# Loading a tile's decays as two DMAs of 64 rows, in a kernel with a written order of work

## What is computed

```python
x = x + 0.5 * _L0_ffn_ref(_layernorm(x), ...)
x = x + _L0_attn_ref(_layernorm(x), ...)
x = x + 0.5 * _L0_ffn_ref(_layernorm(x), ...)
```

```python
C = ft[:, :, None, None] * C + it[:, :, None, None] * (vt[..., :, None] * kt[..., None, :])
n = ft[..., None] * n + it[..., None] * kt
ht = jnp.einsum('bhde,bhe->bhd', C, qt)
denom = jnp.maximum(jnp.abs(jnp.einsum('bhd,bhd->bh', n, qt)), 1.0)[..., None]
```

## Time and profile before

| | |
|---|---|
| time, median of 3 runs | 1038.27 us (1033.71 to 1042.24) |
| profiled execution, its own time | 1040.67 us |
| its span | 1038.6 us |
| mean granted TensorE clock | 0.939 of full speed |
| TensorE busy | 890.4 us (86%) |
| VectorE busy | 627.3 us (60%) |
| ScalarE busy | 358.7 us (35%) |
| GpSimd busy | 244.5 us (24%) |
| DMA queue of SP, share of 16 engines | 25.7% |

### The profile page before, as it was taken

The page is one execution under the profiler, slowest core; times in us unless marked ns, Lnnn a source line. Parts: engine busy times, 40 slices in busy tenths (PEclk is TensorE's granted clock), DMA queues, the critical chain, the costliest instruction groups (busy, mean ns, idle before and its releaser), DMA issues.

```text
span 1038.6 us, 30736 instructions
## 1 busy us (share of the span) xinstructions
PE 890.4 (86%) x12744; PEld 846.2 (81%) x12744; DVE 627.3 (60%) x1502; ACT 358.7 (35%) x716; POOL 244.5 (24%) x234
## 2 busy tenths in 40 slices
PE   3858579998859997998999988799887987699998
PEld 3848568998759996998889988799876976698998
DVE  5454367684826756576666748466574786477742
ACT  5262042432503334242523335143342442123431
POOL 2022123220312202332312213331142043321110
PEclk9978679999989999999999999899898988899999
DMA  8013322213233101322224113331032223330000
GB/s 260 29 37 114 95 82 87 64 54 80 60 104 106 46 19 51 106 90 66 58 69 135 42 54 78 115 89 49 10 98 76 73 85 102 107 91 2 1 12 31
DMA packets 64392, 76.03 MB, mean 73 GB/s; under 512 B 10782, under 2 KB 46750, under 8 KB 64256
## 3 DMA queue, kind: packets, MB, share of 16 engines
q1 hardware_dynamic: 64256, 74.08, 25.7%
HBM read 56.75 MB, written 17.30 MB: 71 GB/s over the span
## 4 chain that ended last, share of the span: by engine, by line
PE 48%; DMA 16%; issue 15%; SPq 8%; DVE 7%; ACT 3%; POOL 2%; ACTq 0%; DVEq 0%; POOLq 0%
PE bank L1092 14%; PE bank L1093 12%; PE bank L1094 12%; DMA dm<-f_scratch 9%; SPq L438 4%; DMA parts_scratch<-pc 2%; DMA arena<-parts_scratch 2%; SPq L456 2%; PE bank L1250 2%; PE bank L1127 2%; DMA f_scratch<-fTz 1%; DMA c_scratch<-cum 1%; PE bank L1310 1%; PE bank L1329 1%; PE bank L1289 1%
## 5 line engine op out<-in xcount | busy, mean ns | idle before, releaser
L1092 PE MATMUL bank<-wo_hi,r_h 128*128 128x256 f32 x512 | 151.2, 295 | 19.4 <-DVE r_l L835 17.4
L643 ACT ACTIVATE r_h<-bank 128x512 fp32r<-128x512 f32 x128 | 76.4, 597 | 252.9 <-PE bank L1127 181.5
L1092 PE MATMUL bank<-xT_hi,wi_hi 128*128 128x256 f32 x512 | 151.2, 295 | 2.5 <-DVE r_l L835 2.4
L1093 PE MATMUL bank<-wo_hi,r_l 128*128 128x256 f32 x512 | 147.2, 288 | 0.0
L1094 PE MATMUL bank<-wo_lo,r_h 128*128 128x256 f32 x512 | 147.1, 287 | 0.0
L1093 PE MATMUL bank<-xT_hi,wi_lo 128*128 128x256 f32 x512 | 146.6, 286 | 0.0
L1094 PE MATMUL bank<-xT_lo,wi_hi 128*128 128x256 f32 x512 | 146.4, 286 | 0.0
L835 DVE SCALAR_TENSOR_TENSOR r_l<-bank,r_h 128x512 fp32r<-128x512 f32 x128 | 87.4, 684 | 87.0 <-ACT r_h L643 86.8
L1012 DVE TENSOR_TENSOR_SCAN dm<-dm,diag 128x512 f32<-128x512 f32 x64 | 78.6, 1229 | 67.2 <-DMA dm<-f_scratch 67.1
L1092 PEld LDWEIGHTS bank<-wo_hi,r_h 128*128 128x128 f32 x512 | 100.0, 195 | 23.4 <-issue 19.8
L1092 PEld LDWEIGHTS bank<-xT_hi,wi_hi 128*128 128x128 f32 x512 | 100.3, 196 | 4.7 <-DVE r_l L835 3.1
(11 more groups left out here) (157 smaller groups left out, 2152.5 us busy)
## 6 DMA issues: line engine op xcount, KB each, us to landing
dm<-f_scratch SPq DMA_DIRECT2D x64, 256.0 KB
arena<-parts_scratch SPq DMA_DIRECT2D x96, 128.0 KB, 3.3
...
x<-in_x SPq DMA_DIRECT2D x16, 256.0 KB, 3.0
...
```

Source lines behind the costliest of these rows:

```text
L643: nc.scalar.activation(flat(r_h[:, n]), U[use % 2][:], ACT.Relu).then_inc(f_rh, 1)
L1092: nc.tensor.matmul(dst, lh, rh, start=first, stop=False, **more)
L1093: nc.tensor.matmul(dst, ll, rh, start=False, stop=False, **more)
```

## The change

E_ issues two DMAs for a unit in place of one. Before, one DMA had a source of 2 rows, each repeated 64 times (2 x 64 x 512), and all 128 partitions as its destination. Now each half `m` is a DMA of its own: the source is the one row of that half, repeated 64 times (64 x 512), and the destination is 64 partitions. Both count 16 on the same semaphore, so that D_ (and F_, which overwrites `f_scratch` two blocks later) waits for 32 a unit where it waited for 16. The bytes are the same, and no other instruction is added or removed.

```diff
@@ F_ (SP)
-                            sp.wait_ge(d_fb[g], 16 * len(range(g, UNITS * (b - 1), DMBUFS)))
+                            sp.wait_ge(d_fb[g], 32 * len(range(g, UNITS * (b - 1), DMBUFS)))
@@ E_ (SP)
-                        src = f_d[b % 2, j, :, GH * g:GH * (g + 1)].rearrange("m h t -> m (h t)")
-                        sp.dma_start(dm[:, n % DMBUFS], src.unsqueeze(1).to_broadcast([2, TH, GH * TH])).then_inc(d_fb[n % DMBUFS], 16)
+                        for m in range(2):
+                            src = f_d[b % 2, j, m, GH * g:GH * (g + 1)].rearrange("h t -> (h t)")
+                            sp.dma_start(dm[TH * m:TH * (m + 1), n % DMBUFS], src.partition_broadcast(TH)).then_inc(d_fb[n % DMBUFS], 16)
@@ D_ (VectorE)
-                    dve.wait_ge(d_fb[n % DMBUFS], 16 * (n // DMBUFS + 1))
+                    dve.wait_ge(d_fb[n % DMBUFS], 32 * (n // DMBUFS + 1))
```

The table ORDER is redrawn for all five engines. Each letter occurs as often as before; most pieces move by a few places. Its first row for SP:

```diff
-        H 7A F X E F C A E 2A E 4K E 2A 2K 2E 2K 2E 6A F E F E C X 2A E K A 2K E K E A E 2A 3K E K 6A E 2A F E F A E A K E 2K C E K 2O X K 2A K E K E K E 7A E
+        H 7A F X F E C E A E A 4K E A E 2A 2K E K E K E 6A F E A K F X 2E 2A C K A K A K 2E A K E 2K E K 7A E A F K A K E F K E A E C O A K O X K A K E 2K 3E
```

More of the change, by code:

```diff
@@ L93 @@
     "PE": """
[L94 to L101, removed]
@@ L102 @@
-        U G U V U M 2U V 2U S V U V U G 2U Y S 2U V G V U V U 2M 2U Y 2U 2Y 3M G S U 2Y S U M G U 2S Y M G U M U Y M G U Y 2U Y V U M 2S M 3U V Y U V U Y U V
-        U Y M S M S G M 2U V U Y 2U Y V Y 2M S V S M V 2U Y G U Y S M S Y M 3U M 2V Y U Y V Y U 3M 2U Y U Y V U V G V U G 4U V U V U V G 3U G U V G U V G U V
-        5U V U V U G U 2V G 3U V 2U G V U G 2U 2V 5U 2V 4U 2V 4U V 2U 3V""",
-    "DVE": """
[L106 to L116, removed]
@@ L117 @@
-    "ACT": """
[L118 to L124, removed]
+        3G U G 5U V 2U V 2U 2V 4U V U V U 2V 2G 5U G U G 2U G U G 7U V 2U V 2U 2V 4U S U V S Y V 2U M 2V M 2S M 2Y M G 2S Y G 3U M 2U M U M Y S U S G 2Y M U G
@@ new lines @@
+        M U G 2U G M Y M 4U Y 2U Y V 2U V M 2U 2V Y U Y 3U V 2U G 2V S G V 4U V 2U V Y U V U G U S M U G U V U G V U G V S 2M S 3U V 2U V 3U 2V 2U Y 2U V 3U V
+        G 2V G U Y U Y U M 3U M S U M G Y U Y M G Y 2S G U S M U M U G 4U Y V Y 3U V U 2M Y S 2V M U Y 2U Y 2U V S 2U G U 3V 2U G 3U V M U V 2U V S G Y M U G
+        S 3U G V U G 2V 4U V 3U M U V U 2V 3U V G U V 2U G Y V U V U Y U Y 3U M S M S M S Y G M U Y M G Y S 2U G M 2U G 3U M Y V 3U Y M U Y V U M V Y 2U Y V U
+        V 3U G U V U V G V 2U 2S U Y 2U V U V U V U G 2U V G U M S U G M S M V G U V 5U 2V 4U 2V 2U G 3U V G V Y U V U V Y 2U Y 3U M 2S 2M S G U Y U Y G M S Y
@@ new lines @@
+        U M G 2U G M 3U Y 3U Y 2U V Y 2M V M U V U Y V 2U Y 2U V U G V U S V U V M 2U G 2U V Y U V U V S U G 2U G V 2U 2S G M V M U G V 4U V 2U V U V U Y V G
+        3U V 3U V U 2V G U Y 3U Y 2U S 3M S G Y M U Y M Y S G U M G U M 2U Y G U S 4U V Y 2U Y V U V 2S 2M 2U Y V U Y V 4U G U V G 2V 4U 2M 2S U V U Y U 2V U
+        G M 2U G U V G S 2U G 2V Y 4U M U 2V 4U 2V U G U V U Y 3U 2V U G V Y U M 4U S M U S Y G U M Y G Y S M G 2U M G 8U V Y V U Y S 2M Y V S M V Y 4U V Y 3U
+        V G V 2U G V 3U V 2U V U M V G 3U Y U G V U 2S M 2V 2U M 2U Y 2U Y M Y M G S M U Y G S Y 2U S M S Y M G U M U Y G M 2U Y U Y V 2U S 2M S V 3U Y V Y V
@@ new lines @@
+        4U M Y 2U 2M 2S V G Y 2U Y V Y 2M 2V 2S M U Y 2U Y G M Y 2U V U S 2M V Y U Y V M S Y U 2M U Y 2U Y V U V G V U G 4U V U V U V G 3U G U V G U V G U V
+        5U 2V 2U V G U V G 4U V G U V U G U V U V 5U V U V U V U V 6U V U 3V""",
+    "DVE": """
+        2G H 3G 3H 2G 3H G H R 2H R 2H 2R H 3R G R 3H 2R H 3G 2H 3G R 2G R G R H 3R G 2R 2H R 2G R H 2R H G 2R 2H 2R D 3R D P R P Y R D G D Y 2R G Y G P Y G D
+        Y P G D 2G R G R Y G P 2R Y G P D 2R Y 2R Y D Y G P Y R P G Y 2R G Y 2R G Y R 2Y 2R D 2G R Y D Y R Y R G Y G R G R G 2R 2G 2R 2G 2R P R G 7R G 2R Y R
+        D R G 2R G R D P 2G 2R P R Y 2G Y R P G 2D 4R D 2R G Y R G R Y 2R Y G Y R G R G R G Y R P Y R G Y R G P Y R Y R G 2R G Y P R Y R D G Y R P R D Y G P R
+        G 2Y R Y D 2G 3R P G 3R D 4R G R G R G R 2G 2R G R P 3R G 2R G 2R Y G 2R G R D Y P R 2G D Y R D R G 2R G R D G R 2G Y 2R G R Y G Y 3R Y R P Y R P Y R
+        G Y R Y G Y 2R G 2R G P Y R Y D P 2G 2R 5Y G R Y R G R G R G R 2D 4R P G R Y R P 3R G R 2G R G 2R D 3R G R D R G R G 2R 2G 2R Y R G 2P G R G R Y D 2R
+        D R G R Y R G D 2R Y R G R Y G R G Y R G R 2P R 2Y G R Y R G Y 2R G 2R G 2Y R Y R P D Y G P Y R D Y R Y R G R G Y 2G R 2D R G P 7R G 3R 2G R 2G Y 3R G
+        2R P G 4R G R D G R P R G R G D G Y R G R Y 3R Y D P 2R G R 2G R G R G Y R G D R Y R Y R Y P R Y P Y G Y 2R Y P G Y 2R G 2R G Y 2R D Y R D G Y P G Y R
+        Y D Y G 2R Y 2G 2R P G 2R P G 2R D 3R D R G 2R G P G R G Y 3R G R Y 2R Y G 2R G 2R G 3R 2G P G D R G R P D 2R Y R Y R D G R G 2R 2G R G R Y R G R Y R
+        Y R D R P Y G R Y G Y R G Y 2R G R P 2R P 2Y R 2Y R G D Y 2D 2R G P Y G P R Y 2G R G R G 5R G R 2G 4R G 6R G D Y R Y 3R P 2G 2R P R Y R D R G R G Y R
+        G 2Y R D R 2Y P G Y D R P Y G Y D Y 2R P G Y R Y G 2R Y P 2Y G R D P Y R G D Y R P D R G Y R 2G 2Y R D Y P Y R P Y D Y R Y G D R Y R Y P R P Y 2R D R
+        G Y R Y 2R Y R G Y P D Y R Y P 2R G Y R G 2R Y R Y G R G 2R G 3R G 3R 2G R G 2R G 4R G 4R G R G 2R G 2R 2G R 2G 2R G 2R G R G 2R G 11R""",
@@ new lines @@
+    "ACT": """
+        H 6G H 2G 6H G 3H 2R 4H 3R H 2R 4H R H 6G 2H 2R 2H R 3G 3R G 2R A R Z G R G A G R G R H 2R 2A Z H G Z 8R Y 6G 3R Z R 2G 4R A 2R Y G A 3G R 2G 2R G 2R
+        Y R 2A 3R Y R G R 4G R G 5R 2G R 2G R G R G R G R Z G 2R G 4R 2G R G R Y 2R 3G 3R 2Z 6R A G R 3G A Y 2G R 2G A 3R G R Y Z 3R Y 2R A 4G R G 2R Z 3R G
+        3R 6G R G R G 3R G Z 4R Z R 2G R G R 3G R Y 3R Z 5R A 2R 3G A Y 3G R 2G 3R 2A G R Y 2R Y 2R 3G R 2G 3R G 2R 2Z 4R Z 4G 2R 2G R 2G 2R G 2R Z R G R G R
+        2G R G R G Y 10R A G R 2G A 3G Y R 2G R A 2R G R Y A 4R Y R G R 4G 4R G 4R 5G R G R 2G 2R Z R G 4R 3G Y 2R 2G 2R G 4R 2G 3R G R A R Z G R Y A G Z G R
+        2G A 3R G Y R A 3R Y R Z R G R 4G R G 7R 6G 2R 2G 2R Z R G R Z 3R 2G R G Y R G Z G 2R G 3R Z 6R A G R 2G Y A 3G R 2G 3R G A R A 2R Y 2R Y 2R 5G R G 6R
+        Z 3G R G 2R Z G R G 6R Y 4R A 2R 3G A 3G Y R 2G R A 2R Y G 2Z A 3R Y 3R 2G Y R 2G Z G Z 2R Y Z 2R G 3R Y 2R Z R Y 3R 5G R G 5R 4G R 2G 2R G R G 2R G
+        3R G R 5G 2R 2G R G 9R""",
@@ L125 @@
     "POOL": """
-        H 4G 2A G A Q A 2W Q W Y W Y G Y W G Y A W A Y 2W G A 2Y Q G Y W G A W 2G W Q Y W G 2Y G 2A Y 2W A 2Y 2W Y W G Q G A W 3G Y Q W Y W G W Y G A Y W A W
-        Y W A 2Y 2G 2W A G Q Y Q W Y G Y 2G 2W Y G 2A W Y G Y W Y W A Y G W A W G W 2G Y 2Q G Y W G Y W A W Y A Y W A W Y G W 2Y W A Q G Q G W G Y G W Y G W Y
-        G W 2A Y G 2Y W A W Y G W G A W G Y Q W Q W G Y A Y W Y A 2W A 2Y G W Y W A Y W Q G Q Y G Y 2W 2Y 3W 2Y W Y 6G""",
+        H 4G 2A G 2A Q 2W Y W Q W Y 2G W Y A W A Y 2W Y A 2Y 2G Q W G W A Y 2G W Y Q Y W G Y 2W G 2A Y G A W Y W 2Y W G Q G Q A G W Y G W Y G W G Y W A Y W A
@@ L129 @@
+        G Y 2W Y A Y G W A Y W Q G Y G 2W Q Y 2G Y G 2A 2W G 3Y W A W Y W A G W G W G Y 2Q W 2G Y G Y A 2W Y A Y W 2A W 2Y 2G W 2Q G Y 2W G Y W Y 3G W Y 2A W
+        3Y W A W A G Y G 2W G Q G Y W Q W Y G A Y A 2W 2Y W Y A W G Y A W Y 2Q W Y G W G Y W Y W Y W Y W Y W Y 6G""",
     "SP": """
-        H 7A F X E F C A E 2A E 4K E 2A 2K 2E 2K 2E 6A F E F E C X 2A E K A 2K E K E A E 2A 3K E K 6A E 2A F E F A E A K E 2K C E K 2O X K 2A K E K E K E 7A E
-        2F A 2E A K O K A C A E O X K E K E A 3K 2E K 7A E K F 3E 3A K O K A F A C O X K E K 2E 2K E K 6A E K A F 2A 2E A K F 2K E C O E O K X 2A K 3E 2K E 7A
@@ L132 @@
-        F K 2A E K A 2E 2K O A K F E A K E C E K E K 5A E 2A K 2A O F K 2E K A F E A C A K E 2K 2E O 2K 2E 5O""",
+        H 7A F X F E C E A E A 4K E A E 2A 2K E K E K E 6A F E A K F X 2E 2A C K A K A K 2E A K E 2K E K 7A E A F K A K E F K E A E C O A K O X K A K E 2K 3E
+        6A F 2E F C 3A O A E K E K O K X E K E K 2A K 2E 2K 6A F E A K E 2A K A E O E K F E K O X 2A C 2K E K 2E K 6A K 3A F K E A E K 2E F K O C 2A K O E X
+        2E K E 2K E 6A K A F A E A K A 2E F C O 2K 2A K 2E K E 2K 2A E 3A E 2A F K 3A E K F E C A 2E 2K E O K A E 3K O 2E 5O""",
```

## The result

| | before | after |
|---|---|---|
| time, median | 1040.26 us (4 runs, 1033.71 to 1043.10) | 935.10 us (4 runs, 934.78 to 939.06) |
| ratio, 95% interval | | 0.9006, 0.8954 to 0.9057 |
| span of the profiled execution | 1038.6 us | 936.9 us |
| TensorE busy / idle | 890.4 / 148.2 us | 865.0 / 71.9 us |
| mean granted clock | 0.939 | 0.980 |

The account below looks back on a forecast made before the run. TensorE's idle time and lower clock, caused by decay loads on two of sixteen DMA engines, were taken as the bound. 1040.7 - 19 - 31 - 18 + 8 = 981 for the profiled execution, so 978 us forecast, range 942 to 1012.

Parts of the forecast that it names:

- Step 1: Decay loads into dm: both halves run on 16 engines and land in 3.9 us, against 8.73 alone or 17.39 queued.
- rival of the one source row: Decay loads: one row limits the rate whatever the engines, a load takes 14 us, kernel 1096 us; chance 0.05.
- rival of the serializing halves: Decay loads: each half gets only the old engines, so the pair takes 9.3 us, kernel 1050 us; chance 0.05.
- Steps 2 and 3: TensorE's idle gaps: 19 us from S_ waits for arena, 31 us from nine gaps behind VectorE's waits for decays.
- the next releaser: TensorE's nine gaps behind decay waits: another wait follows closely, so 1 us was left at each.
- Step 4: TensorE's work at half clock behind eleven gaps, 43.2 us: up to 21.6 us come back, 18 taken.
- Step 5: SP's queue: 64 more issues, 34 us on SP alone, mostly hidden by its waiting; full 34 if cover were gone.
- Step 6: Redrawn instruction order, most pieces moved a few places: a loss of 8 us, bounds 16 gained to 40 lost.
- more than forecast: Whole kernel: the redrawn order fills what fast loads leave, all marked gaps and 16 us more go, 937 us; chance 0.12.

Follow-up runs that it names:

- e6_outer4: After, with the 64 repeats of each half's one source row written as 4 x 16; 952.8 us, ratio 0.9169 to before.
- e6_outer8: After, with the 64 repeats of each half's one source row written as 8 x 8; 937.1 us, ratio 0.9019 to before.
- e1_loads_only: After with the ORDER table of before, so only the split loads differ from before; 944.5 us, ratio 0.9080.
- e8_one_wide: After with one 128-row load a unit from 16 source rows, each half's row stored 8 times; 939.1 us, ratio 0.9057 to before.
- e7_beside: After plus, behind each unit's two loads, one DMA of the old 2 x 64 shape into a spare DRAM buffer; 1025.9 us, ratio 0.9900 to before.
- e4_rows_48_16: After with each half cut again into 48 and 16 rows, four DMAs a unit; 935.4 us, ratio 0.9021 to before.

## Why the prediction was right in direction and wrong in size

**Step 1, the load.** Right. Share 0.12 to 0.14 at an outer size of 2, proportional up to 8; landing 3.6 us for the pair against 3.9. That after has all 16 engines, as the step says, stays unproven. The rival of the one source row is dead: `e6_outer4` and `e6_outer8` read one row with 4 and 8 engines and the share grows in step. So is the rival of the serializing halves: `e1_loads_only` takes 944.5 us where before takes 1040.9. The Trainium skill's rule against two transfers to disjoint partition halves (DMA: Bandwidth & Descriptors, "Rules for kernel authors") supposes that either half is spread over all 16 engines, and so is the one transfer in its place; here the one had two. Where the one is wide, the rule fits: `e8_one_wide` (939.1) and after (935.1) are the same within their intervals. With the Trainium skill's rule on the number of engines (same page, "Why a DMA increments its semaphore by 16 and not by 1") the traces agree: 0.14, 0.25 and 0.48 for outer sizes of 2, 4 and 8, and 0.12 for 62 rows. Two of the rivals' sums are off by 2 us: 1040 + 48 + 10 is 1098 and not 1096, and 1040 + 7 + 5 is 1052 and not 1050. Nothing hangs on it.

**Steps 2 and 3, the idle time.** Mis-sized: I forecast 19 + 31 = 50 us and `e1_loads_only`, which has the old order, gained 68.9 over its whole span. The gaps that I had marked were 26.6 + 40.2 = 66.8. The marking was right, and the discounts were not: the 8 us taken off the S_ gaps and the 9 us left at nine gaps for "the next releaser". Looked up one by one, the three S_ gaps lost 25.6 us in place of 19, and the nine others 39.1 in place of 31; 2.1 us are left where I had left 17. So no next releaser stood behind the decays that would have held TensorE up by more than 1 us. The other 4.3 us lie in gaps that I had not marked; what gave them is open, though `e7_beside` shows that two held engines can delay the stores of the parts too (SP's wait for `pc`), which no gap carried by name.

**Step 4, the clock.** Mis-sized: 18 us forecast, 27.0 measured (busy time, `e1_loads_only`). I took 43.2 us of TensorE's work behind eleven gaps and then a sixth off the 21.6 they promise. But behind 100 us TensorE did 76.9 us of work at the lower level, and 16.3 in `e1_loads_only`: 60.6 us moved up. The rest of them lay behind small gaps that I had not marked (472, 523 and 905 us, behind gaps of 2.2, 2.4 and 1.5) and around the start of the first attention (131 us). The mean clock says the same: 0.939 over 1038.6 us is 127 us at the lower level, idle time included (twice the missing 0.061), and 0.980 over 942.7 is 38.

**Step 5, SP's issues.** Right in that they are hidden, and too careful: I had given 3 us back for them in step 2. 128 further issues cost nothing clear of the noise (935.4 us in `e4_rows_48_16`, 935.1 in after, on another chip).

**Step 6, the order.** Wrong in sign: I took a loss of 8 us; it gained 9.4 with the wide loads (8 by the ratios, 0.9080 and 0.9006, from two chips) and 12.8 with the narrow, on one chip (0.9884, 0.9869 to 0.9899). In the profiles of after and `e1_loads_only` it is idle time (71.9 against 79.3 us). Which of the moved pieces it was is open; no run separates them.

The three misses are 19 (idle), 9 (clock) and 17 (order), 45 us together, and 981 less 45 is 936. All pointed the same way, because I had set a discount at each step. The rival "more than forecast" had taken them off and came to 937, but not by its mechanism: it has the new order fill what the loads leave, and `e1_loads_only` gained 96 of the 105 us in the old order. Its 16 us of other gaps measured 4 for the loads and 8 to 9 for the order, and its 21.6 for the clock 27. That the sum meets to 2 us is partly luck.
